# Pair columns inside an eight-field part laid out by halves, in a DLRM tower with a compressed-interaction layer

## The chip, the cores and the metric

The kernel runs on one core of a Trainium2 chip. The metric is the device time of one execution in microseconds (us). The kernel before took 377.16 us (median of 3 runs, 375.65 to 377.16).

## What is computed

For each of 1024 samples 32 rows of 32 numbers are gathered from 32 tables. From these `e` the interaction network forms products of pairs and contracts them with weights twice; the sums over the last axis go through a tower of three dense layers.

```python
e = stack([tbl_f[ids[:, f]] for f in range(32)], axis=1)     # (1024, 32, 32)
x, res = e, []
for W in (W0, W1):                                           # (1024, 128), (4096, 128)
    z = einsum('bhd,bmd->bhmd', e, x).reshape(b, 32 * x.shape[1], 32)
    x = einsum('bpd,pj->bjd', z, W)
    res.append(x)
z = sum(concatenate(res, axis=1), axis=-1)                   # (1024, 256)
h = maximum(concatenate([z, dense_ctx], 1) @ W_top1 + b_top1, 0)
h = maximum(h @ W_top2 + b_top2, 0)
y = h @ W_top3
```

All is float32.

## The kernel before

The product of field a with field b is the same as that of b with a, so the kernel works on unordered pairs, each with the sum of its two weights. The 32 fields are two sides of 16 (`HALF`), and each side two parts of 8 (`SUB`); there are four parts. The 28 pairs inside a part are 28 columns of a block of 32 (`PAIRS`), and four squares fill it up; `pair_columns` names the field pair of every column. Pairs that cross the two parts of a side have 64 columns, those that cross the sides 256 more.

**Weights.** TensorE multiplies W1, row block by row block, with the summed W0 columns (`sym`), for each of 32 fields h: 272 columns into `RT[h]`, 256 into `RX[h]` (ScalarE copies them out of PSUM). What is needed is a sum over the orders of a triple of fields, so DVE adds shifted pieces of `RX` or `RT` into `RT`, and into `QC` and `TH`, by the helper `add` (line 421, `tensor_tensor` with both inputs in SBUF). `own_adds` handles triples within a side (both inputs in `RT`), `apart_across` one part of side X against the other side, `both_across` both parts at once, `cross_first` and `cross_second` the 64 crossing columns. Each is called twice, with a first and a second round (`second`), since the second adds to what the first wrote. Then TensorE transposes the result into `C` (`weights`).

**Gathers.** GpSimd (POOL) issues 256 indirect DMAs (line 278), 8 for each of 32 units of 32 samples, one behind the other; they wait only for the index rows and for a buffer of two tiles before.

**Units.** For each unit TensorE transposes the gathered rows into the PSUM bank `ET` (`emb_transposes`), ScalarE copies `ET` to `eblk` and `eT`, DVE forms the products in `products` in three parts (`zQ` across parts, `zP` inside parts, `z3` the rest; one input is `ET` in PSUM, the other `eT` in SBUF), and TensorE contracts them (`triples`, `across_triples`, `other_triples`). ScalarE and DVE copy those results to `TS`; TensorE multiplies them with `C` (`second`, line 726). Every four units make a tile of 128 samples, and the tower follows behind each.

**Order.** Each engine's program is written out by hand, and semaphores tie them. On DVE: the first two units' products, `own_sums(0)`, `early_sums`, and then for each unit its copies, the next unit's products and, for the first three, one part of `late_sums`.

In the products inside a part, distance by distance: instruction s multiplies the fields i and i + s, for 8 - s values of i, over all parts and samples of the unit. `off(s)` is the first column of distance s. The sums go over the same columns in the same order, by distances; one more instruction does the squares in the first round.

Of the kernel before, what the change touches and what calls it, by code (L numbers as in the profile page):

```python
# [7 lines left out]
ALU = mybir.AluOpType  # L8
ACT = mybir.ActivationFunctionType

P = 128
# [3 lines left out]
HALF = 16  # L15
SUB = 8
# [7 lines left out]
Y1T = 7  # L24


def off(s):

    return sum(SUB - r for r in range(1, s))


def pair_columns():


    cols = [None] * RTC
    for p in range(4):
        f0 = SUB * p
        for s in range(1, SUB):
            for i in range(SUB - s):
                cols[32 * p + off(s) + i] = (f0 + i, f0 + i + s)  # L40
        for i in range(4):
            cols[32 * p + PAIRS + i] = (f0 + i, f0 + i)
            cols[2 * P + 4 * p + i] = (f0 + 4 + i, f0 + 4 + i)
    for X in range(2):
        for i in range(SUB):
            for k in range(SUB):
                cols[P + 64 * X + SUB * i + k] = (HALF * X + i, HALF * X + SUB + k)
    return cols


def dlrm_cin_tower(nc, dense_t, ids, bases, table, w_top1, w_dense, vec_in, w_top2, w0_cols, w0_rows, w1, out):
# [21 lines left out]
    C17 = HALF + 1  # L73
    EB = NQ * 2 * C17
    N1, N2 = H1 // P, H2 // P
    NZ = 11
    W1P = 8
    KT = 56

# [1 line left out]
    with ctx:  # L81
# [9 lines left out]
        def view(t, at, dims):  # L91

            return bass.AP(t.tensor, t.offset + at, [list(t.ap[0])] + [list(d) for d in dims])
# [325 lines left out]
        def _(eng):  # L419
            def add(dst, a, b, s):  # L420
                eng.tensor_tensor(dst, a, b, ALU.add).then_inc(s, 1)

            def rt(h, col, dims):
                return view(RT[:, :, :], RTC * h + col, dims)

            def rx(X, h, c, other, by_c, by_h, by_other):
# [2 lines left out]
                dims = [[to_c, by_c]] + [[RAB * a + to_other * b, n] for a, b, n in zip(by_h[0::2], by_other, by_h[1::2])]  # L429
                return view(RX[:, :, :], RAB * (HALF * X + h) + to_c * c + to_other * other, dims)  # L430

            def th(c, x, dims):
                return view(TH[:, :, :], THIRD * c + x, dims)

            def apart_across(X, e, c0, cn, second, s_done):

                for s in range(1, SUB) if second else range(0, SUB):  # L440
                    n = SUB - s if s else 4
                    dst = rt(HALF * (1 - X) + c0, 32 * (2 * X + e) + (off(s) if s else PAIRS), [[RTC, cn], [1, n]])
                    h, other = (s, 0) if second else (0, s)
                    add(dst, dst, rx(X, SUB * e + h, c0, SUB * e + other, cn, (1, n), (1,)), s_done)

            def both_across(X, c0, cn, second, s_done):

                for s in range(1, SUB) if second else range(0, SUB):
                    n = SUB - s if s else 4
                    dst = rt(HALF * (1 - X) + c0, 64 * X + (off(s) if s else PAIRS), [[RTC, cn], [32, 2], [1, n]])  # L450
                    h, other = (s, 0) if second else (0, s)
                    add(dst, dst, rx(X, h, c0, other, cn, (SUB, 2, 1, n), (SUB, 1)), s_done)

            def cross_first(X, c0, cn, s_done):

# [8 lines left out]
            def own_adds(X, e, second):  # L464


                f, c = (SUB, 1) if e == 0 else (1, SUB)
                for s in range(1, SUB) if second else range(0, SUB):
                    n = SUB - s if s else 4
                    dst = rt(HALF * X + SUB * (1 - e), 32 * (2 * X + e) + (off(s) if s else PAIRS), [[RTC, SUB], [1, n]])  # L470
                    h, other = (s, 0) if second else (0, s)
                    add(dst, dst, rt(HALF * X + SUB * e + h, P + 64 * X + f * other, [[c, SUB], [RTC + f, n]]),
                        (own_added if second else own_first)[X])

            def rest_across(X):

# [15 lines left out]
            def own_sums(X):  # L492
                for e in range(2):
                    own_adds(X, e, False)
                eng.wait_ge(own_first[X], 2 * SUB)
                for e in range(2):
                    own_adds(X, e, True)

            def early_sums():


                eng.wait_ge(rt_kept, HALF + SUB)
                eng.wait_ge(rx_kept, (HALF + SUB) // 2)
                both_across(0, 0, SUB, False, early_first)
                cross_first(0, 0, SUB, early_first)
                apart_across(1, 0, 0, HALF, False, early_first)
                cross_first(1, 0, HALF, late_first)
                eng.wait_ge(early_first, 2 * SUB + 1)
                both_across(0, 0, SUB, True, added)
                cross_second(0, 0, SUB, added)  # L510
                apart_across(1, 0, 0, HALF, True, added)

            def late_sums(part):
                if part == 0:
                    eng.wait_ge(rt_kept, F)
                    eng.wait_ge(rx_kept, F // 2)
                    both_across(0, SUB, SUB, False, late_first)
                    cross_first(0, SUB, SUB, late_first)
                    apart_across(1, 1, 0, HALF, False, late_first)
                    for X in range(2):  # L520
                        rest_across(X)
                        rest_own(X)
                        rest_same(X)
                if part == 1:
                    own_sums(1)
                if part == 2:
                    eng.wait_ge(late_first, 2 * SUB + 2)
                    both_across(0, SUB, SUB, True, added)
                    cross_second(0, SUB, SUB, added)
                    apart_across(1, 1, 0, HALF, True, added)  # L530
                    cross_second(1, 0, HALF, added)
# [7 lines left out]
            def products(u, part):  # L539

                parts, sides = 4 * GROUPS, 2 * GROUPS
                within, across, rest = zP[u % 2][:, :, :], zQ[u % 2][:, :, :, :], z3[u % 2][:, :, :]

                def apart(s):
                    some = [[SUB, parts], [1, SUB - s]]
                    eng.tensor_tensor(view(within, off(s), [[32, parts], [1, SUB - s]]), field(0, some), copied(s, some),  # L546
                                      ALU.mult).then_inc(z_made, 1)

                if part == 0:
                    eng.wait_ge(eblk_made, (NQ + 1) * (u + 1))  # L550
                    wait(eng, t3_made, u - 1)
                    eng.tensor_tensor(view(across, 0, [[64, sides], [SUB, SUB], [1, SUB]]),  # L552
                                      field(0, [[HALF, sides], [1, SUB], [0, SUB]]),
                                      copied(SUB, [[HALF, sides], [0, SUB], [1, SUB]]), ALU.mult).then_inc(z_made, 1)
                if part == 1:
                    for s in range(1, 5):
                        apart(s)
                if part == 2:
                    for s in range(5, SUB):
                        apart(s)  # L560
                    some = [[SUB, parts], [1, 4]]
                    eng.tensor_tensor(view(within, PAIRS, [[32, parts], [1, 4]]), field(0, some), copied(0, some),
                                      ALU.mult).then_inc(z_made, 1)
                    some = [[F, GROUPS], [SUB, 4], [1, 4]]
                    eng.tensor_tensor(view(rest, 0, [[THIRD, GROUPS], [4, 4], [1, 4]]), field(4, some), copied(4, some),
                                      ALU.mult).then_inc(z_made, 1)
                    eng.tensor_copy(view(rest, MORE, [[THIRD, GROUPS], [1, HALF]]), field(0, [[F, GROUPS], [1, HALF]]))\
                       .then_inc(z_made, 1)
# [64 lines left out]
        def _(eng):  # L633
# [14 lines left out]
            def weights(q):  # L648

                bank = WA[:, :] if q % 2 else M[:, :, :].rearrange("p a b -> p (a b)")  # L650
                if q == 0:
                    eng.wait_ge(added, 4 * (SUB - 1) + 9)
                    for X in range(2):
                        eng.wait_ge(own_added[X], 2 * (SUB - 1))
                wait(eng, c_kept, q - 1)
                for x in range(4):
                    kt = 4 * q + x
                    if kt < F:
                        piece = RT[:, kt, 0:P]
                    elif kt < F + HALF:  # L660
                        piece = QC[:, kt - F, :]
                    else:
                        n = 4 * (kt - F - HALF)
                        piece = TH[:, n:n + 4, :].rearrange("p c x -> p (c x)")
                    m = eng.transpose(bank[:, P * x:P * x + P], piece, ident[:, :])
                m.then_inc(c_made, 1)
# [209 lines left out]
```

## Time and profile before

| what | us |
|---|---|
| median of 3 runs | 377.16 |
| the profiled execution's own time | 377.52 |
| its span | 375.7 |
| PE busy (matmul) | 323.7 |
| POOL busy | 252.3 |
| ACT busy | 233.9 |
| DVE busy | 203.2 |

The span runs from the first to the last instruction. The page and the timeline give each instruction by its line, its engine and its tiles, with the elements per partition; starts are counted from the span's start. DVE instructions overlap: the next starts before the length given for one is over, so the step from start to start is what one costs. A row of the timeline with "x8" is a merged run of eight. The granted clock of TensorE was 0.982 of full speed over the span.

### The profile page before, as it was taken

The page shows a single profiled execution, that of the slowest core. Times are in us where ns is not written, and L with a number is a line of the kernel's source. Part 1 is how long each engine was busy: PE and PEld are TensorE (multiplying, and loading weights), DVE is VectorE, ACT ScalarE, POOL GpSimd, SP SyncE. Part 2 cuts the span into 40 slices and gives each one's busy share as a digit, 9 for nine tenths or more (in the row PEclk, how much of TensorE's full clock was granted, in tenths as well). Part 3 has the DMA queues.
Part 4 walks back from the last instruction along what each step waited for, and adds up shares of the span by engine and source line. Part 5 has one row for each costly group of instructions (what it writes and reads, how often), then busy time and mean ns, then how long its engine had stood idle before and what let it go on. Part 6 is the DMA issues. An engine that isn't in the chain of part 4 may idle for free.

```text
span 375.7 us, 11560 instructions
## 1 busy us (share of the span) xinstructions
PE 323.7 (86%) x4680; PEld 298.8 (80%) x4680; DVE 203.2 (54%) x834; ACT 233.9 (62%) x774; POOL 252.3 (67%) x262
## 2 busy tenths in 40 slices
PE   1899936249998999899989998998699879989897
PEld 1677735248998999899989988988698878889797
DVE  4336999933665565555646663655455544554201
ACT  1578566187667766776686667666676557556601
POOL 5777887877777777777777777777777777740000
PEclk9999996699999999999999999999999999999999
DMA  7801001010100010000101000100010001100000
GB/s 220 312 14 16 11 9 16 9 16 14 16 16 16 14 16 16 16 16 15 16 13 17 15 17 15 15 15 15 15 16 14 16 15 17 15 10 2 3 2 0
DMA packets 10773, 9.79 MB, mean 26 GB/s; under 512 B 4664, under 2 KB 8896, under 8 KB 10720
## 3 DMA queue, kind: packets, MB, share of 16 engines
q0 software_dynamic: 8192, 4.21, 7.5%
q1 hardware_dynamic: 2528, 4.84, 3.8%
q8 instruction: 37, 0.61, 0.7%
q14 instruction: 16, 0.13, 0.1%
HBM read 9.03 MB, written 0.00 MB: 24 GB/s over the span
## 4 chain that ended last, share of the span: by engine, by line
POOL 66%; issue 21%; PE 10%; DMA 1%; ACT 1%; POOLq 0%; DVE 0%; SPq 0%
POOL emb L278 66%; PE WA L726 4%; PE M L739 1%; PE PA L687 1%; DMA emb<-in_table,rows 1%; PE QB L698 1%; DMA base<-in_bases 1%; PE M L758 1%; PE M L749 0%; POOLq L81 0%; ACT h L358 0%; PE T L711 0%; PE T L787 0%; PE M L750 0%; PE ET L787 0%
## 5 line engine op out<-in xcount | busy, mean ns | idle before, releaser
L278 POOL DMA_INDIRECT emb<-in_table,rows x256 | 251.6, 983 | 80.4 <-issue 77.8
L726 PE MATMUL WA<-TS,RX 128*128 128x128 f32 x896 | 111.0, 277 | 1.0 <-ACT TS L285 1.0
L726 PEld LDWEIGHTS WA<-TS,RX 128*128 128x128 f32 x896 | 104.6, 192 | 4.1 <-issue 4.0
L584 DVE COPY TS<-T 32x64 f32<-32x64 f32 x256 | 55.5, 217 | 76.7 <-PE T L711 69.7
L285 ACT ACTIVATE eblk<-ET 32x256 f32<-32x256 f32 x128 | 48.7, 380 | 55.3 <-PE ET L674 53.0
L687 PE MATMUL PA<-eblk,zP 128*128 128x132 f32 x512 | 75.0, 282 | 1.9 <-ACT TS L285 1.1
L552 DVE TENSOR_TENSOR zQ<-ET,eT 128x1024 f32<-128x1024 f32 x32 | 39.2, 1225 | 65.2 <-ACT eT L285 65.1
L285 ACT ACTIVATE TS<-T 32x64 f32<-32x64 f32 (+1 forms) x320 | 66.5, 208 | 7.7
L687 PEld LDWEIGHTS PA<-eblk,zP 128*128 128x128 f32 x512 | 66.7, 195 | 2.7 <-ACT TS L285 1.3
L546 DVE TENSOR_TENSOR zP<-ET,eT 128x224 f32<-128x224 f32 (+6 forms) x224 | 47.7, 289 | 0.0
L285 ACT ACTIVATE TS<-PA 128x396 f32<-128x396 f32 (+1 forms) x96 | 44.5, 463 | 2.7 <-PE PA L687 1.6
L698 PE MATMUL QB<-eblk,zQ 128*32 128x68 f32 x2048 | 37.5, 224 | 0.0
L698 PEld LDWEIGHTS QB<-eblk,zQ 128*32 128x32 f32 x2048 | 32.1, 109 | 4.0 <-issue 0.2
L639 PE MATMUL PA<-sym,TS 128*128 128x272 f32 x64 | 21.2, 415 | 8.9 <-DMA TS<-in_W 7.7
L711 PE MATMUL T<-eblk,z 128*32 128x132 f32 x512 | 20.8, 279 | 4.8 <-DVE TS L587 3.5
L674 PE MATMUL ET<-ident,emb 128*128 128x128 f32 x64 | 13.4, 293 | 12.2 <-DMA emb<-in_table,rows 9.5
L285 ACT ACTIVATE TS<-QB 128x272 f32<-128x272 f32 x64 | 22.1, 408 | 0.0
L758 PE MATMUL M<-h,wt 128*128 128x128 f32 x112 | 14.4, 281 | 8.7 <-ACT h L358 8.7
L639 PEld LDWEIGHTS PA<-sym,TS 128*128 128x128 f32 x64 | 12.2, 198 | 11.3 <-issue 7.6
L758 PEld LDWEIGHTS M<-h,wt 128*128 128x128 f32 x112 | 13.0, 191 | 10.1 <-ACT h L358 10.1
L285 ACT ACTIVATE RT<-PA 128x272 f32<-128x272 f32 x32 | 12.6, 395 | 13.3 <-PE PA L639 13.2
L674 PEld LDWEIGHTS ET<-ident,emb 128*128 128x128 f32 x64 | 7.7, 146 | 15.1 <-DMA emb<-in_table,rows 11.8
(87 smaller groups left out, 290.5 us busy)
## 6 DMA issues: line engine op xcount, KB each, us to landing
emb<-in_table,rows POOLq DMA_INDIRECT x256, 2.4
TS<-in_W SPq DMA_DIRECT2D x8, 256.0 KB, 5.6
wt<-in_W_top SPq DMA_DIRECT2D x2, 512.0 KB, 8.3
y1w<-in_W_rows SPq DMA_DIRECT2D x1, 448.0 KB, 6.7
TS<-in_W_rows SPq DMA_DIRECT2D x1, 448.0 KB, 7.3
sym<-in_W_cols SPq DMA_DIRECT2D x1, 264.0 KB, 3.0
TS<-in_W_cols SPq DMA_DIRECT2D x1, 264.0 KB, 3.3
idc<-in_ids SPq DMA_DIRECT2D x1, 128.0 KB, 2.1
```

The source lines that it names most:

```text
L278: eng.indirect_dma_start(emb[par][:, g, :], None, table, bass.IndirectOffsetOnAxis(rows[:, k, g:g + 1], 0))\
L285: return eng.activation(dst, src, ACT.Copy)
L546: eng.tensor_tensor(view(within, off(s), [[32, parts], [1, SUB - s]]), field(0, some), copied(s, some), ALU.mult).then_inc(z_made, 1)
L552: eng.tensor_tensor(view(across, 0, [[64, sides], [SUB, SUB], [1, SUB]]), field(0, [[HALF, sides], [1, SUB], [0, SUB]]), copied(SUB, [[HAL ...
L584: eng.tensor_copy(view(ts[32 * q:32 * q + 32, :, :], P * REST + b0, [[4 * P, 2], [P, 4], [1, 8]]), view(src, q, [[C17, 2], [4, 4], [C33, 8 ...
L639: eng.matmul(PA[h % 2][:, 0:RTC], w1s[:, h, :], sym[:, 0:RTC], start=True, stop=True).then_inc(rt_made, 1)
L674: t = eng.transpose(ET[:, P * q:P * q + P], emb[k % 2][:, g:g + NQ, :].rearrange("p g d -> p (g d)"), ident[:, :])
L687: m = eng.matmul(PA[t % 2][:, NQ * C33 * x:NQ * C33 * x + NQ * C33].rearrange("p (v c) -> p v c", c=C33), zP[u % 2][:, g, :], eblk[u % 2][ ...
L698: m = eng.matmul(QB[g // 4][32 * j:32 * j + 32, at:at + NQ * C17].rearrange("p (v c) -> p v c", c=C17), zQ[u % 2][:, g, X, y0:y0 + 32], eb ...
L711: m = eng.matmul(T3[32 * j:32 * j + 32, at:at + NQ * C33].rearrange("p (v c) -> p v c", c=C33), z3[u % 2][:, g, :], eblk[u % 2][:, g, :, 1 ...
L726: m = eng.matmul(WA[:, 0:P], C[:, kt, :], TS[k % 2][:, slot_of(kt), :], start=(kt == 0), stop=(kt == KT - 1))
L758: m = eng.matmul(M[:, a, :], wt2[:, c, cols], h1[:, c, :], start=(c == 0), stop=(c == N1 - 1))
```

## The change

The 28 columns of a part are laid out in another order: 16 pairs of the fields 0 to 3 with 4 to 7, then 4 pairs of the fields 0, 1 with 2, 3, and 4 of 4, 5 with 6, 7, then the four neighbour pairs (0, 1), (2, 3), (4, 5), (6, 7). Each of these four groups is one instruction (a table `BLOCKS` gives the start column, first field and width), where the order by distances takes seven. The host lays out the weights by the same `pair_columns`. In `both_across` the pattern of a group of width 4 or 2 has no dimension left for the two parts, so these stand in a loop over parts. The count `NZ` of a unit's product instructions goes from 11 to 8, and the counts that are waited for change with it.

```diff
-def off(s):
-    return sum(SUB - r for r in range(1, s))
+def part_pairs():
+    pairs = [(a, 4 + b) for a in range(4) for b in range(4)]
+    pairs += [(4 * n + a, 4 * n + 2 + b) for n in range(2) for a in range(2) for b in range(2)]
+    pairs += [(2 * j, 2 * j + 1) for j in range(4)]
+    return pairs
...
-    NZ = 11
+    NZ = 8
+    BLOCKS = ((0, 0, 4), (HALF, 0, 2), (HALF + 4, 4, 2), (HALF + SUB, 0, 1))
...
+            def steps(w, by_first, by_second):
+                if w == 1:
+                    return [[2 * (by_first + by_second), 4]]
+                return [[by_first, w], [by_second, w]]
+
+            def pairs_at(w):
+                return [[1, 4]] if w == 1 else [[w, w], [1, w]]
+
             def apart_across(X, e, c0, cn, second, s_done):
-                for s in range(1, SUB) if second else range(0, SUB):
-                    n = SUB - s if s else 4
-                    dst = rt(HALF * (1 - X) + c0, 32 * (2 * X + e) + (off(s) if s else PAIRS), [[RTC, cn], [1, n]])
-                    h, other = (s, 0) if second else (0, s)
-                    add(dst, dst, rx(X, SUB * e + h, c0, SUB * e + other, cn, (1, n), (1,)), s_done)
+                to_c, to_other = (1, HALF) if X == 0 else (HALF, 1)
+                row, col = HALF * (1 - X) + c0, 32 * (2 * X + e)
+                for at, f, w in BLOCKS:
+                    dst = rt(row, col + at, [[RTC, cn]] + pairs_at(w))
+                    h, other = (f + w, f) if second else (f, f + w)
+                    by = (to_other, RAB) if second else (RAB, to_other)
+                    add(dst, dst, rx_at(X, SUB * e + h, c0, SUB * e + other, [[to_c, cn]] + steps(w, *by)), s_done)
+                if not second:
+                    dst = rt(row, col + PAIRS, [[RTC, cn], [1, 4]])
+                    add(dst, dst, rx_at(X, SUB * e, c0, SUB * e, [[to_c, cn], [RAB + to_other, 4]]), s_done)
...
             def both_across(X, c0, cn, second, s_done):
...
+                    if w == 1:
+                        dst = rt(row, col + at, [[RTC, cn], [32, 2]] + pairs_at(w))
+                        add(dst, dst, rx_at(X, h, c0, other, [[to_c, cn], [SUB * (RAB + to_other), 2]] + steps(w, *by)), s_done)
+                    else:
+                        for e in range(2):
+                            dst = rt(row, col + 32 * e + at, [[RTC, cn]] + pairs_at(w))
+                            add(dst, dst, rx_at(X, SUB * e + h, c0, SUB * e + other, [[to_c, cn]] + steps(w, *by)), s_done)
...
                 if part == 1:
-                    for s in range(1, 5):
-                        apart(s)
+                    eng.tensor_tensor(view(within, 0, [[32, parts], [4, 4], [1, 4]]), field(0, [[SUB, parts], [1, 4], [0, 4]]),
+                                      copied(4, [[SUB, parts], [0, 4], [1, 4]]), ALU.mult).then_inc(z_made, 1)
+                    for g in (0, 4):
+                        eng.tensor_tensor(view(within, HALF + g, [[32, parts], [2, 2], [1, 2]]), field(g, [[SUB, parts], [1, 2], [0, 2]]),
+                                          copied(g + 2, [[SUB, parts], [0, 2], [1, 2]]), ALU.mult).then_inc(z_made, 1)
                 if part == 2:
-                    for s in range(5, SUB):
-                        apart(s)
+                    eng.tensor_tensor(view(within, HALF + SUB, [[32, parts], [1, 4]]), field(0, [[SUB, parts], [2, 4]]),
+                                      copied(1, [[SUB, parts], [2, 4]]), ALU.mult).then_inc(z_made, 1)
```

`own_adds` is changed like `apart_across`.

On DVE, in `early_sums`, the instructions of one part across the sides (`apart_across(1, 0, ...)`, the `128x16...` rows) stood between the two `cross_first` (the `...x64` rows) like this before:

```order
L421 TENSOR_TENSOR RT<-RT,RX 128x8x64
L421 TENSOR_TENSOR RT<-RT,RX 128x16x4
L421 TENSOR_TENSOR RT<-RT,RX 128x16x7
L421 TENSOR_TENSOR RT<-RT,RX 128x16x6
L421 TENSOR_TENSOR RT<-RT,RX 128x16x5
L421 TENSOR_TENSOR RT<-RT,RX 128x16x4
L421 TENSOR_TENSOR RT<-RT,RX 128x16x3
L421 TENSOR_TENSOR RT<-RT,RX 128x16x2
L421 TENSOR_TENSOR RT<-RT,RX 128x16
L421 TENSOR_TENSOR RT<-RT,RX 128x16x64
```

In the changed program the same place, with the eight instructions of `both_across` ahead of it (the `128x8...` rows), reads:

```order
L425 TENSOR_TENSOR RT<-RT,RX 128x8x16 x2
L425 TENSOR_TENSOR RT<-RT,RX 128x8x4 x4
L425 TENSOR_TENSOR RT<-RT,RX 128x8x2x4 x2
L425 TENSOR_TENSOR RT<-RT,RX 128x8x64
L425 TENSOR_TENSOR RT<-RT,RX 128x16x16
L425 TENSOR_TENSOR RT<-RT,RX 128x16x4 x4
L425 TENSOR_TENSOR RT<-RT,RX 128x16x64
```

Eight instructions of 112 down to 16 elements became one of 256 and four of 64; nothing else moved between them.

On DVE, a unit's products before (`zQ` across parts, `zP` inside, `z` the rest):

```order
L552 TENSOR_TENSOR zQ<-ET,eT 128x1024
L546 TENSOR_TENSOR zP<-ET,eT 128x32x7
L546 TENSOR_TENSOR zP<-ET,eT 128x32x6
L546 TENSOR_TENSOR zP<-ET,eT 128x32x5
L546 TENSOR_TENSOR zP<-ET,eT 128x32x4
L546 TENSOR_TENSOR zP<-ET,eT 128x32x3
L546 TENSOR_TENSOR zP<-ET,eT 128x32x2
L546 TENSOR_TENSOR zP<-ET,eT 128x32
L562 TENSOR_TENSOR zP<-ET,eT 128x32x4
L565 TENSOR_TENSOR z<-ET,eT 128x8x16
L567 COPY z<-ET 128x8x16
```

and in the changed program:

```order
L584 TENSOR_TENSOR zQ<-ET,eT 128x1024
L588 TENSOR_TENSOR zP<-ET,eT 128x32x16
L591 TENSOR_TENSOR zP<-ET,eT 128x32x4 x2
L594 TENSOR_TENSOR zP<-ET,eT 128x32x4
L597 TENSOR_TENSOR zP<-ET,eT 128x32x4
L600 TENSOR_TENSOR z<-ET,eT 128x8x16
L602 COPY z<-ET 128x8x16
```

Seven instructions with 896 elements became four with the same 896.

## Rows read from the trace of the kernel before

**Rows 1.** The page: the chain that ended last, and the costliest group.

```profile
POOL emb L278 66%; PE WA L726 4%; PE M L739 1%; PE PA L687 1%; DMA emb<-in_table,rows 1%; PE QB L698 1%; DMA base<-in_bases 1%; PE M L758 1%; PE M L749 0%; POOLq L81 0%; ACT h L358 0%; PE T L711 0%; PE T L787 0%; PE M L750 0%; PE ET L787 0%
...
L278 POOL DMA_INDIRECT emb<-in_table,rows x256 | 251.6, 983 | 80.4 <-issue 77.8
```

**Rows 2.** The gathers' own line: duration min/median/max, first and last start.

```profile
L278 POOL DMA_INDIRECT emb<-in_table,rows x256: 943/947/2323, 4.1 to 332.5; - x128
```

**Rows 3.** Timeline, end of the gathers: start, length, engine, operation, [idle before].

```profile
332.50 0.95 POOL L278 DMA_INDIRECT emb<-in_table,rows  x1 [0.31 <-issue]
334.90 0.44 PE L674 MATMUL ET<-ident,emb 128*128 128x128 f32 x2 [1.03 <-DMA emb<-in_table,rows]
...
338.55 1.49 DVE L546 TENSOR_TENSOR zP<-ET,eT 128x224 f32<-128x224 f32 x7
...
340.34 0.28 DVE L567 COPY z<-ET 128x128 f32<-128x128 f32 x1
...
343.58 0.84 PE L687 MATMUL PA<-eblk,zP 128*128 128x132 f32 x6
```

**Rows 4.** Timeline, middle of the run: a unit's last gather, and its transposes.

```profile
192.43 0.95 POOL L278 DMA_INDIRECT emb<-in_table,rows  x1 [0.30 <-issue]
...
198.78 0.38 PE L674 MATMUL ET<-ident,emb 128*128 128x128 f32 x2
```

**Rows 5.** Line of the transposes from 200 us on: what PE idled for, us, times.

```profile
  DMA emb<-in_table,rows: 8.1, 9
```

**Rows 6.** Groups of POOL's instructions between 30 and 80 us: busy, mean ns, idle.

```profile
L278 POOL DMA_INDIRECT emb<-in_table,rows x34 | 40.9, 1204 | 10.4 <-issue 10.4
```

**Rows 7.** Timeline of POOL: seven of the slow gathers.

```profile
5.52 1.45 POOL L278 DMA_INDIRECT emb<-in_table,rows  x1 [0.30 <-issue]
...
37.68 1.69 POOL L278 DMA_INDIRECT emb<-in_table,rows  x1 [0.31 <-issue]
...
41.21 1.97 POOL L278 DMA_INDIRECT emb<-in_table,rows  x1 [0.30 <-issue]
43.48 2.11 POOL L278 DMA_INDIRECT emb<-in_table,rows  x1 [0.30 <-issue]
...
49.78 2.12 POOL L278 DMA_INDIRECT emb<-in_table,rows  x1 [0.30 <-issue]
...
69.06 2.32 POOL L278 DMA_INDIRECT emb<-in_table,rows  x1 [0.30 <-issue]
71.69 1.59 POOL L278 DMA_INDIRECT emb<-in_table,rows  x1 [0.30 <-issue]
```

**Rows 8.** Timeline of DVE, windows cut so that single instructions and blocks stand.

```profile
5.44 0.71 DVE L594 TENSOR_TENSOR sym<-sym,TS 128x528 f32<-128x528 f32 x1 [1.61 <-DMA TS<-in_W_cols]
...
34.68 4.04 DVE L421 TENSOR_TENSOR RT<-RT 128x32 f32<-128x32 f32 x30
...
38.63 1.53 DVE L421 TENSOR_TENSOR RT<-RT,RX 128x64 f32<-128x64 f32 x8
...
40.09 1.03 DVE L421 TENSOR_TENSOR RT<-RT,RX 128x512 f32<-128x512 f32 x1
...
42.25 0.22 DVE L421 TENSOR_TENSOR RT<-RT,RX 128x32 f32<-128x32 f32 x1
42.38 0.17 DVE L421 TENSOR_TENSOR RT<-RT,RX 128x16 f32<-128x16 f32 x1
42.48 1.21 DVE L421 TENSOR_TENSOR RT<-RT,RX 128x1024 f32<-128x1024 f32 x1
43.62 1.36 DVE L421 TENSOR_TENSOR RT<-RT,RX 128x112 f32<-128x112 f32 x7
...
44.80 0.17 DVE L421 TENSOR_TENSOR RT<-RT,RX 128x16 f32<-128x16 f32 x1
44.89 1.11 DVE L421 TENSOR_TENSOR QC<-RT,RX 128x512 f32<-128x512 f32 x1
...
70.57 1.88 DVE L421 TENSOR_TENSOR QC<-RT,RX 128x1024 f32<-128x1024 f32 x1
```

More of the change, by code:

```diff
@@ L37, in pair_columns @@
         f0 = SUB * p
-        for s in range(1, SUB):
-            for i in range(SUB - s):
-                cols[32 * p + off(s) + i] = (f0 + i, f0 + i + s)
+        for n, (a, b) in enumerate(part_pairs()):
+            cols[32 * p + n] = (f0 + a, f0 + b)
         for i in range(4):
@@ L430, in rx, with rx_at @@
                 return view(RX[:, :, :], RAB * (HALF * X + h) + to_c * c + to_other * other, dims)
+            def rx_at(X, h, c, other, dims):
+                to_c, to_other = (1, HALF) if X == 0 else (HALF, 1)
+                return view(RX[:, :, :], RAB * (HALF * X + h) + to_c * c + to_other * other, dims)
             def th(c, x, dims):
                 return view(TH[:, :, :], THIRD * c + x, dims)
-            def apart_across(X, e, c0, cn, second, s_done):
-                for s in range(1, SUB) if second else range(0, SUB):
-                    n = SUB - s if s else 4
-                    dst = rt(HALF * (1 - X) + c0, 32 * (2 * X + e) + (off(s) if s else PAIRS), [[RTC, cn], [1, n]])
-                    h, other = (s, 0) if second else (0, s)
-                    add(dst, dst, rx(X, SUB * e + h, c0, SUB * e + other, cn, (1, n), (1,)), s_done)
@@ L446, in both_across @@
-            def both_across(X, c0, cn, second, s_done):
[L448 to L452, printed above, removed]
+            def steps(w, by_first, by_second):
+                if w == 1:
+                    return [[2 * (by_first + by_second), 4]]
+                return [[by_first, w], [by_second, w]]
@@ new lines, in pairs_at @@
+            def pairs_at(w):
+                return [[1, 4]] if w == 1 else [[w, w], [1, w]]
+            def apart_across(X, e, c0, cn, second, s_done):
+                to_c, to_other = (1, HALF) if X == 0 else (HALF, 1)
+                row, col = HALF * (1 - X) + c0, 32 * (2 * X + e)
[7 more added lines that the diff above has]
+                    add(dst, dst, rx_at(X, SUB * e, c0, SUB * e, [[to_c, cn], [RAB + to_other, 4]]), s_done)
@@ new lines, in both_across @@
+            def both_across(X, c0, cn, second, s_done):
+                to_c, to_other = (1, HALF) if X == 0 else (HALF, 1)
+                row, col = HALF * (1 - X) + c0, 64 * X
+                for at, f, w in BLOCKS:
+                    h, other = (f + w, f) if second else (f, f + w)
+                    by = (to_other, RAB) if second else (RAB, to_other)
+                    if w == 1:
[5 more added lines that the diff above has]
+                            add(dst, dst, rx_at(X, SUB * e + h, c0, SUB * e + other, [[to_c, cn]] + steps(w, *by)), s_done)
+                if not second:
+                    dst = rt(row, col + PAIRS, [[RTC, cn], [32, 2], [1, 4]])
+                    add(dst, dst, rx_at(X, 0, c0, 0, [[to_c, cn], [SUB * (RAB + to_other), 2], [RAB + to_other, 4]]), s_done)
@@ L467, in own_adds @@
                 f, c = (SUB, 1) if e == 0 else (1, SUB)
[L468 to L473, printed above, removed]
+                row, col, s_done = HALF * X + SUB * (1 - e), 32 * (2 * X + e), (own_added if second else own_first)[X]
+                for at, g, w in BLOCKS:
+                    h, other = (g + w, g) if second else (g, g + w)
+                    by = (f, RTC) if second else (RTC, f)
+                    dst = rt(row, col + at, [[RTC, SUB]] + pairs_at(w))
+                    add(dst, dst, rt(HALF * X + SUB * e + h, P + 64 * X + f * other, [[c, SUB]] + steps(w, *by)), s_done)
+                if not second:
+                    dst = rt(row, col + PAIRS, [[RTC, SUB], [1, 4]])
+                    add(dst, dst, rt(HALF * X + SUB * e, P + 64 * X, [[c, SUB], [RTC + f, 4]]), s_done)
             def rest_across(X):
@@ L494, in own_sums @@
                     own_adds(X, e, False)
-                eng.wait_ge(own_first[X], 2 * SUB)
+                eng.wait_ge(own_first[X], 2 * 5)
                 for e in range(2):
@@ L507, in early_sums @@
                 cross_first(1, 0, HALF, late_first)
-                eng.wait_ge(early_first, 2 * SUB + 1)
+                eng.wait_ge(early_first, 8 + 1 + 5)
                 both_across(0, 0, SUB, True, added)
@@ L526, in late_sums @@
                 if part == 2:
-                    eng.wait_ge(late_first, 2 * SUB + 2)
+                    eng.wait_ge(late_first, 1 + 8 + 1 + 5)
                     both_across(0, SUB, SUB, True, added)
@@ L542, in products @@
                 within, across, rest = zP[u % 2][:, :, :], zQ[u % 2][:, :, :, :], z3[u % 2][:, :, :]
[L544 to L547, printed above, removed]
                 if part == 0:
@@ L651, in weights @@
                 if q == 0:
-                    eng.wait_ge(added, 4 * (SUB - 1) + 9)
+                    eng.wait_ge(added, 2 * 7 + 2 * 4 + 9)
                     for X in range(2):
-                        eng.wait_ge(own_added[X], 2 * (SUB - 1))
+                        eng.wait_ge(own_added[X], 2 * 4)
                 wait(eng, c_kept, q - 1)
```

## The prediction

> **What bounds the kernel now.** I read the page's chain of waits first: 66% of the span is the issue of the gathers on POOL, line 278 [rows 1]. The 256 gathers start between 4.1 and 332.5 us; one takes 0.947 us by the median, but the slowest 2.32 [rows 2], and 0.30 of idle lies between two [rows 7]. So 1.25 us each is the pace, and the last gather starts at 332.50. The timeline at that end shows TensorE idle 1.03 us for it, its transposes at 334.90, and then work on PE without a hole that the changed engine makes [rows 3]. From there to the end of the span is 375.7 - 334.9 = 40.8 us of TensorE work that the diff doesn't touch.
>
> Is TensorE near enough to become the bound if gathers come earlier? In the middle of the run it is late: the gather that ended at 193.38 got its transposes at 198.78 [rows 4]. From 200 us on it has caught up, and idles 8.1 us in 9 waits for gathers [rows 5]. So gathers may come some 8 us earlier and the end follows one for one; if they come later, it follows at once.
>
> DVE doesn't set the end by its own length: the last unit's products end at 340.34 + 0.28 = 340.62, and PE first needs them at about 343.6 [rows 3], 2.9 us later. **DVE matters through another door.** Between 30 and 80 us there are 34 gathers with 40.9 us busy [rows 6]; at the median it would be 34 x 0.947 = 32.2. These 8.7 us are nearly all of the excess of the run (251.6 - 256 x 0.947 = 9.2, [rows 1]). The slow ones stand where DVE does the additions of line 421 [rows 7, 8].
>
> When does a slow gather get on? The addition of 5.44 us ends at 6.15, the gather that began inside it at 6.97 [rows 7, 8]: 0.82 after. Take 0.82 off the ends of the gathers of 41.21, 43.48 and 69.06, and each falls beside the start of a DVE addition: 42.36 (a start at 42.38), 44.77 (44.80) and 70.56 (70.57). For the first two the instruction just ended has 32 elements a partition, for the last 16; the gather of 43.48 has by then let pass the boundaries behind 112, 96, 80, 64 and 48 elements, all of one block of seven [rows 7, 8]; the gather of 71.69 waits for the end of the 1024, 72.45, behind which a copy from PSUM comes. So a waiting gather gets in only behind a short addition or behind one that doesn't read SBUF twice. Behind 32 elements it is not always so: the gather of 69.06 passes the one behind 32 and gets in behind 16, at the start of the 1024 (70.57).
>
> The Trainium skill, "SBUF — State Buffer", section "SBUF: two separate sides", says that a VectorE instruction with two SBUF inputs and a GpSimd operation that reads SBUF exclude each other for the whole instruction, whichever starts first. That they exclude each other, the trace agrees; but by that rule alone the gather of 43.48 would go on at the next boundary, after about 0.1 us, and it took 2.11 us in place of 0.947 [rows 7]. A run of additions back to back keeps the port here, so I price the change by lengths of runs. What it would be by the rule stands as a rival.
>
> **Price of an addition.** Seven instructions, 448 elements, from 43.62 to 44.89: 1.27 us; one of 16 elements, from 42.38 to 42.48: 0.10 [rows 8]. Solving gives about 0.065 us an instruction and 0.0018 us an element with strided inputs. The 1024 contiguous from 42.48 to 43.62: 1.14, so 0.00105 an element [rows 8].
>
> **The change, part by part.**
> - Products: 11 instructions of a unit become 8, elements unchanged: 3 x 0.065 = 0.2 us in each of 32 units, 6.2 us of DVE. All of it lies beside waits: in the last unit the cover is the 2.9 us above. Price 0. If the new patterns (stride 0 inside four, stride 2) ran at 0.0018 in place of 0.00105, the 896 elements cost 0.7 more and are still covered. If the cover were gone, the last unit would give -0.2 or cost up to 0.5.
> - Own sums: 30 instructions to 18 in each half; they take 34.68 to 38.63, 3.95 us [rows 8], so 12 x 0.065 = 0.8 less, twice.
> - Sums of one part across (four blocks, two with eight instructions and two with seven): to five and four. First: 8 x 0.065 + 512 x 0.0018 = 1.44; now 5 x 0.065 + 256 x 0.00105 + 256 x 0.0018 = 1.05, since the 4 by 4 and 2 by 2 read neighbours. Second: 1.26 to 1.07. Together 1.2 us less.
> - Sums of both parts across: eight and seven instructions before and after, same elements: 0. But sizes change from 64, 112 down to 16, to two of 128, four of 32, one or two of 64.
> - No wait is added; the counts that are waited for follow the new numbers of instructions.
>
> So the additions shrink by about 2.8 us. By itself this moves nothing on the path; the port does. In the new order no addition of 16 or 8 elements is left. Within a block of both parts there are four of 32 in a row; within a block of one part only 256 and 64s; the products by halves (512, 1024) follow right behind.
>
> **Walk through the new stretch**, taking that a gather gets in behind 32 but not behind 64. Own sums start at 34.5 and end at 37.65, with so many of 32 that they hold up a gather little. Then: two of 128 to 38.25, four of 32 to 38.7, 64s to 39.1, 512 (0.96) to 40.05, one part to 41.1, 1024 to 42.25, 128s to 42.8, 32s to 43.3, 64 to 43.5, 512 to 44.5, one part to 45.6, 128s to 46.2, 32s to 46.7, 64s, 512 and one part to 49.05, the rest to the first copy at 49.5. Gathers get in at about 38.5, 42.95, 46.3 and 49.5: three steps in 11.0 us, where the pace asks 3.75, so 7.2 lost. Before, in the same work, the gathers from that of 37.68 to that of 49.78 (three more stand between those shown) get in from 38.55 to 51.08 [rows 7]: six steps in 12.5 us, 5.0 lost. The last part: one gets in among the 32s, the next only at the end behind one part and the 1024, 4.2 us later: 3.0 lost; before, 2.1 (69.06 and 71.69: 1.37 and 0.64, a third 0.1) [rows 7]. The own sums: before 8.7 - 5.0 - 2.1 = 1.6; after, by my choice, half of it, 0.8, since they have so many 32s. Sum 11.0 against 8.7: +2.3 us.
>
> The profiled execution took 377.52; 379.8 with this. The median of the runs lies 0.36 lower, 377.16, so I forecast **379.5 us**. Its own range, by the phase in which gathers meet the runs (one step is 1.25) and by 32 not always letting one in: 377.5 to 382.
>
> **Rivals.**
> 1. *Shorter additions, shorter lock.* The loss goes with the time of the additions: they took 17.4 in one stretch from 34.68 us, 3.95 for the second own sums and, by the prices above, 1.27 + 1.04 + 1.26 + 1.8 = 5.4 in the last part, 26.7 us in all for 8.7 lost, 0.32 each; 2.8 less give -0.9: 376.3. For it: the simplest reading. Against: the ends that fall behind short ones.
> 2. *Behind 64 too.* In the walk gathers then get in also within the blocks of one part (near 40.6, 45.2, 48.6, and 66.7 in the last part): 6.4 lost, -2.3: 375. Against: in the blocks of [rows 7, 8] none did. With every boundary open, as the whole-instruction rule has it, about 4.3 are lost, -4.4: 373. That is the lower end.
> 3. *Only behind 24 or less, on the other side further out.* Then nothing opens the run between 37.7 and 49.5 us, nor that of the last part: one gather in 11.8 us, 10.5 lost, 4 in the last part, 2 in the own sums: +7.8, 385. It decides if a waiting gather lets pass most of the 32s; the gather of 69.06 did once, two others didn't.
> 4. *DVE's own time counts*: 32 x 0.2 = 6.2 us less, 371. Against: the 2.9 us of cover and the gathers' pace.
>
> **How the numbers follow.** Forecast 0.42, of it 0.1 ends within 0.5%; rival 1 0.18; rival 2 with every boundary 0.20; rival 3 0.18; rival 4 0.02. A measurement of this kernel tells 0.5%, 1.9 us, from no change. Faster 0.22, same 0.18 + 0.10 = 0.28, slower 0.50. The range, from every boundary open to nothing behind 32: 373.3 to 385.5; the likeliest's own is given above.
>
> **What would show it.** The gathers' line between 30 and 80 us: fewer than 34 starts, mean above 1204 ns, single ones of 3 us and more near 39 to 42 and 65 to 69; their ends less 0.82 behind additions of 32. The start of the last gather near 334.8, transposes 2.4 later, and still 40.8 to the end. The adds of one part at 1.05 us, a unit's within-part products near 1.2. I am wrong if the last gather starts before 332.5, if gathers get in behind 64s or 256s, or if the tail behind the last transposes changes.

## The result, and the profile after

| | before | changed |
|---|---|---|
| median, us | 377.09 (375.65 to 377.16, 4 runs) | 383.46 (380.15 to 384.21, 4 runs) |
| profiled execution, its own time and span | 377.52, 375.7 | 383.21, 381.4 |
| last gather starts | 332.50 | 338.22 |
| 256 gathers busy, less 256 x 0.947 | 9.2 | 15.0 |

The ratio is 1.016, 95% interval 1.012 to 1.020: 6.4 us slower. The bound is the same and is later. The page of the changed kernel, the chain and the gathers' group (the lines that answer to [rows 1]):

```profile
POOL emb L282 67%; PE WA L761 4%; PE M L774 1%; PE PA L722 1%; DMA emb<-in_table,rows 1%; PE QB L733 1%; DMA base<-in_bases 1%; PE M L793 1%; PE M L784 0%; POOLq L85 0%; ACT h L362 0%; PE T L746 0%; PE T L822 0%; PE M L785 0%; PE ET L822 0%
...
L282 POOL DMA_INDIRECT emb<-in_table,rows x256 | 257.4, 1005 | 80.3 <-issue 77.7
```

The timeline at the end of the gathers, to be held against [rows 3] (start, length, engine, operation, [idle before]):

```profile
338.22 0.94 POOL L282 DMA_INDIRECT emb<-in_table,rows  x1 [0.30 <-issue]
...
340.55 0.44 PE L709 MATMUL ET<-ident,emb 128*128 128x128 f32 x2 [0.97 <-DMA emb<-in_table,rows]
...
344.21 0.68 DVE L588 TENSOR_TENSOR zP<-ET,eT 128x512 f32<-128x512 f32 x1
...
345.80 0.28 DVE L602 COPY z<-ET 128x128 f32<-128x128 f32 x1
...
349.25 0.84 PE L722 MATMUL PA<-eblk,zP 128*128 128x132 f32 x6
```

The last gather is 5.72 us later, the transposes 5.65, and from them to the end are 381.4 - 340.55 = 40.85 us, where it was 40.8. The products of the last unit end 0.2 us sooner after the transposes than before, and PE needs them 3.2 us later: nothing of that is seen at the end. So the whole loss lies in when the gathers were issued. Between 30 and 80 us (against [rows 6]) there are five gathers fewer, and the mean is longer:

```profile
L282 POOL DMA_INDIRECT emb<-in_table,rows x29 | 42.4, 1464 | 8.8 <-issue 8.8
```

That is 42.4 - 29 x 0.947 = 14.9 us lost there, where it was 8.7. The timeline of POOL in the stretch of the sums (against [rows 7]):

```profile
36.00 1.36 POOL L282 DMA_INDIRECT emb<-in_table,rows  x1 [0.30 <-issue]
37.66 6.57 POOL L282 DMA_INDIRECT emb<-in_table,rows  x1 [0.30 <-issue]
44.53 5.81 POOL L282 DMA_INDIRECT emb<-in_table,rows  x1 [0.30 <-issue]
50.65 0.95 POOL L282 DMA_INDIRECT emb<-in_table,rows  x1 [0.30 <-issue]
...
64.54 4.96 POOL L282 DMA_INDIRECT emb<-in_table,rows  x1 [0.30 <-issue]
```

and DVE there, merged runs (against [rows 8]):

```profile
34.98 2.98 DVE L425 TENSOR_TENSOR RT<-RT 128x128 f32<-128x128 f32 x18
37.87 5.83 DVE L425 TENSOR_TENSOR RT<-RT,RX 128x128 f32<-128x128 f32 x22
43.62 1.06 DVE L425 TENSOR_TENSOR QC<-RT,RX 128x512 f32<-128x512 f32 x1
44.59 4.47 DVE L425 TENSOR_TENSOR RT<-RT,RX 128x256 f32<-128x256 f32 x18
48.98 0.36 DVE L425 TENSOR_TENSOR TH<-RT,RX 128x128 f32<-128x128 f32 x1
49.26 0.26 DVE L425 TENSOR_TENSOR TH<-RT 128x64 f32<-128x64 f32 x1
49.44 0.18 DVE L526 COPY TH<-RT 128x64 f32<-128x64 f32 x1
...
66.77 1.90 DVE L425 TENSOR_TENSOR QC<-RT,RX 128x1024 f32<-128x1024 f32 x1
68.57 0.94 DVE L619 COPY TS<-T 32x64 f32<-32x64 f32 x4
```

The reader is to see three gathers of 5 to 6.6 us (three more took 1.0 to 1.4) where the kernel before had thirteen slow ones of 1.0 to 2.3. The end of each less 0.82 is where it gets on, as in the prediction. These are 43.41, 49.52 and 68.68: the first behind the last of four additions of 32 elements (a step of 0.149 where the other three take 0.12), the second at the end of a copy, the third when the 1024 is over and a copy from PSUM comes. DVE itself became shorter, as was worked out: own sums 2.9 us for 3.95, the stretch to the first copy from PSUM 15.15 us (34.98 to 50.13) for 17.5.

From the instruction starts of five traces (the kernel before, the changed one in two profiles, and the two below that add short additions) I counted, for each gather later than 30 us that waited, which addition had just ended when it got in, and which ends it let pass.

| elements of the addition just ended | let pass | got in |
|---|---|---|
| 8 | 0 | 14 |
| 16 | 1 | 6 |
| 24 | 2 | 1 |
| 32, contiguous inputs (a step of 0.10 to 0.13) | 4 | 9 |
| 32, strided inputs, kernel before | 7 | 3 |
| 32, strided inputs, the four other traces | 55 | 4 |
| 40 to 1024, an addition following | 163 | 1 |

("Contiguous" are the additions of 32 that one experiment below adds; "strided" are all of the sums. Of the four entries in the last but one row, one was at a wait for a semaphore. Entries behind a 1024 that a copy from PSUM follows are left out of the last row.)

### The profile page after: what moved, and what is told of

The parts are those of the page before. It is cut to its first block, busy times and chain, and to the rows that moved or that the text cites. A ratio compares the mean times of both kernels' runs of the same rounds, so it can differ in the third digit from the quotient of the medians.

```text
span 381.4 us, 11428 instructions
## 1 busy us (share of the span) xinstructions
PE 327.9 (86%) x4680; PEld 301.6 (79%) x4680; DVE 192.7 (51%) x702; ACT 234.1 (61%) x774; POOL 258.0 (68%) x262
## 4 chain that ended last, share of the span: by engine, by line
POOL 67%; issue 21%; PE 10%; DMA 1%; ACT 1%; POOLq 0%; DVE 0%; SPq 0%
POOL emb L282 67%; PE WA L761 4%; PE M L774 1%; PE PA L722 1%; DMA emb<-in_table,rows 1%; PE QB L733 1%; DMA base<-in_bases 1%; PE M L793 1%; PE M L784 0%; POOLq L85 0%; ACT h L362 0%; PE T L746 0%; PE T L822 0%; PE M L785 0%; PE ET L822 0%
## 5 line engine op out<-in xcount | busy, mean ns | idle before, releaser
L282 POOL DMA_INDIRECT emb<-in_table,rows x256 | 257.4, 1005 | 80.3 <-issue 77.7
L722 PE MATMUL PA<-eblk,zP 128*128 128x132 f32 x512 | 75.9, 284 | 1.9 <-ACT TS L289 1.1
L722 PEld LDWEIGHTS PA<-eblk,zP 128*128 128x128 f32 x512 | 67.5, 197 | 2.7 <-ACT TS L289 1.5
L588 DVE TENSOR_TENSOR zP<-ET,eT 128x512 f32<-128x512 f32 x32 | 21.8, 681 | 0.0
```

Source lines behind the costliest of these rows:

```text
L282: eng.indirect_dma_start(emb[par][:, g, :], None, table, bass.IndirectOffsetOnAxis(rows[:, k, g:g + 1], 0))\
L588: eng.tensor_tensor(view(within, 0, [[32, parts], [4, 4], [1, 4]]), field(0, [[SUB, parts], [1, 4], [0, 4]]), copied(4, [[SUB, parts], [0, ...
L722: m = eng.matmul(PA[t % 2][:, NQ * C33 * x:NQ * C33 * x + NQ * C33].rearrange("p (v c) -> p v c", c=C33), zP[u % 2][:, g, :], eblk[u % 2][ ...
```

## The experiments

All times are medians beside runs of the kernel before on the same chip; "lost" is the gathers' busy time on the page less 256 x 0.947.

| kernel | median, us | ratio to before, interval | lost |
|---|---|---|---|
| changed, memset behind each addition | 372.49 | 0.987 (0.983 to 0.991) | 4.5 |
| before, memset behind each addition | 370.14 | 0.981 (0.977 to 0.985) | 1.0 |
| changed, additions are memsets | 368.24 | 0.977 (0.973 to 0.980) | 0.6 |
| before, additions are memsets | 368.68 | 0.978 (0.974 to 0.981) | 0.7 |
| changed, memset behind each block | 373.24 | 0.988 (0.981 to 0.995) | 4.9 |
| changed, addition of 8 behind each block | 374.60 | 0.994 (0.990 to 0.998) | 5.9 |
| changed, addition of 32 behind each block | 377.45 | 0.999 (0.995 to 1.003) | 10.2 |
| changed, additions are copies | 373.57 | 0.989 (0.982 to 0.996) | 5.3 |
| changed, memsets and crossings cut | 369.86 | 0.979 (0.976 to 0.982) | 1.2 |
| before, memset behind each block | 373.29 | 0.988 (0.984 to 0.991) | 3.8 |
| changed, again | 382.64 | 1.010 (1.006 to 1.015) | 15.6 |

**An opening behind each addition.** The edit, the same in both kernels:

```diff
+            def door():
+                at = next(doors)
+                eng.memset(spare[:, at:at + 1], 0.0)
...
                 eng.tensor_tensor(dst, a, b, ALU.add).then_inc(s, 1)
+                door()
```

> The changed kernel with a memset of one element (no SBUF input) behind each addition of the sums; nothing else is changed. Theory (back-to-back additions with two SBUF inputs keep the port, and a gather gets in behind anything that isn't one): no gather waits longer than the addition it meets, so none takes above 0.95 + 1.9 us; all together they lose 3 to 5 us in place of 15, the last gather starts near 327 to 329 us, time 370.5 to 373. Rival (the gathers lose in proportion to the time that DVE spends on the sums): DVE's stretch becomes some 6 us longer, so 384 or more. Rival (the loss comes from something else in the new layout): 383, unchanged.

> The kernel before with the same memset behind each of its additions. Theory: loss 3 to 5 us in place of 8.7, last gather near 327 to 329, time 371 to 373.5. Rival (in proportion to DVE's time): about 140 more instructions, 379 or more. Rival (the layout alone makes the difference): 377, unchanged.

DVE of the changed kernel with memsets, from its timeline:

```profile
38.31 0.20 DVE L432 TENSOR_TENSOR RT<-RT,RX 128x32 f32<-128x32 f32 x1
38.32 0.06 DVE L429 MEMSET spare<- 128x1 f32 x1
38.44 0.20 DVE L432 TENSOR_TENSOR RT<-RT,RX 128x32 f32<-128x32 f32 x1
38.45 0.06 DVE L429 MEMSET spare<- 128x1 f32 x1
38.57 0.20 DVE L432 TENSOR_TENSOR RT<-RT,RX 128x32 f32<-128x32 f32 x1
```

and its gathers:

```profile
38.65 0.95 POOL L283 DMA_INDIRECT emb<-in_table,rows  x1 [0.30 <-issue]
39.91 1.17 POOL L283 DMA_INDIRECT emb<-in_table,rows  x1 [0.30 <-issue]
41.38 1.85 POOL L283 DMA_INDIRECT emb<-in_table,rows  x1 [0.31 <-issue]
43.54 1.03 POOL L283 DMA_INDIRECT emb<-in_table,rows  x1 [0.30 <-issue]
```

More instructions and less time, in both kernels, as the theory had it. The changed kernel came out inside its expectation: 372.49 us, 4.5 lost, the last gather at 327.68, the longest 2.52 us. The 4.5 are also near the 4.3 that the prediction's rival 2 had worked out for every boundary open. The memset starts 0.01 us after the addition, and the step from one addition of 32 to the next is 0.13 with it, 0.125 without: an opening costs DVE next to nothing. What is left is lost at the long additions: a gather started inside five of the changed kernel's six of 512 and 1024 elements, and these five gathers took 1.17 to 2.52 us.

The kernel before with memsets was faster than expected (370.14 for 371 to 373.5), and lost 1.0 for the 3 to 5 expected, with the same six long additions. There each of the six began 0.14 to 0.44 us after a gather had, and that gather took 0.94 to 0.97; the next one came in the last 0.2 us of the addition or behind it and took 1.08 at most, but for one of 1.61. Two gathers and the addition between them:

```profile
45.66 0.95 POOL L279 DMA_INDIRECT emb<-in_table,rows  x1 [0.30 <-issue]
45.80 1.08 DVE L428 TENSOR_TENSOR QC<-RT,RX 128x512 f32<-128x512 f32 x1
46.91 1.08 POOL L279 DMA_INDIRECT emb<-in_table,rows  x1 [0.30 <-issue]
```

So the 3.5 us between the two losses lie in how the gathers' starts fell against the long additions, in one profile of each kernel. Whether the layout makes them fall so, or chance, isn't shown. The last gather of the kernel before with memsets starts at 324.25, but its span is 369.2, 45.0 later and not 43.2: TensorE no longer waits for gathers (its waits for them are 1.2 us in one, where the changed kernel with memsets has 5.2 in six), its last transposes begin 4.2 us after the last gather (328.48) with PE busy ahead of them, and it has become the bound.

**No SBUF inputs at all.** In both kernels:

```diff
-                eng.tensor_tensor(dst, a, b, ALU.add).then_inc(s, 1)
+                eng.memset(dst, 0.0).then_inc(s, 1)
```

> The changed kernel in which every addition of the sums is a memset of the same output (same number of instructions, same semaphores, no SBUF input; the weights that are computed are left out by this). Theory: no gather is slow behind 30 us, the last starts near 324, time 367.5 to 369.5. Rival (the products' new patterns or a later TensorE cost something too): more than 370, and more than its twin from the kernel before.

> The kernel before in which every addition of the sums is a memset of the same output (the weights that are computed are left out by this). Theory: 367.5 to 369.5, and within 0.5 us of the changed kernel with memsets, so that the port is the whole difference of the two kernels and the products give nothing. Rival (the shorter products are worth something and the port hid it): the changed one with memsets is 1 to 6 us faster than this one.

Between 30 and 80 us, the group of gathers of the changed kernel with memsets for additions (busy, mean ns, idle; against [rows 6]):

```profile
L282 POOL DMA_INDIRECT emb<-in_table,rows x41 | 38.8, 946 | 12.5 <-issue 12.5
```

and of its twin from the kernel before:

```profile
L278 POOL DMA_INDIRECT emb<-in_table,rows x41 | 38.7, 944 | 12.5 <-issue 12.5
```

With their instructions in the same order and no contention the two kernels are 0.4 us apart, which their runs don't separate (367.90 to 368.92 and 368.24 to 368.88), and no gather behind 30 us is slow. So the contention is the whole difference between them as far as these runs can tell, and the shorter products of 32 units give nothing like the 6.2 us of DVE time that they save. One caution for what follows: TensorE was granted a clock of 0.995 in both of these profiles, where it was 0.982 in those of the two kernels and 0.968 to 0.977 in the five with memsets between additions. So 368 us says when the gathers would let the kernel end, and not how fast TensorE would be with real weights.

**Openings behind blocks, of three kinds.** The memset, or instead of it an addition with both inputs in SBUF (`ident`), behind each of the 22 blocks of the changed kernel:

```diff
+            def door():
+                at = 8 * next(doors)
+                eng.tensor_tensor(spare[:, at:at + 8], ident[:, 0:8], ident[:, 32:32 + 8], ALU.add)
```

(with 32 in place of each 8 in the third kernel, and `eng.memset(spare[:, at:at + 1], 0.0)` in the first).

> The changed kernel with the one-element memset only behind each of the 22 blocks of additions (one part, both parts, own, or one crossing product), not behind each addition. Theory (what counts is the length of a run of additions back to back): a waiting gather gets in at the next block's end, 1 to 1.8 us away at most where it was 5; lost 5 to 8 us in place of 15, time 374 to 377. Rival (the memset helps by something other than ending a run, for instance because it delays each addition): in proportion to the memsets, 22 of 116, about 381.

> The changed kernel with one addition of 8 elements, both inputs in SBUF, into a spare tile behind each of the 22 blocks. Theory as in the prediction (a short addition lets a waiting gather in): about as with memsets at the same places, 374 to 378. Rival (only an instruction that doesn't read two SBUF inputs opens the run, and the short additions of the kernel before stood there by chance): 383 to 384.

> The same with 32 elements in place of 8. Theory (short means 16 or less; in the changed kernel gathers passed over a dozen additions of 32): 382 to 385, as without it. Rival (any addition with contiguous operands, or one more instruction, opens the run): 374 to 378, as with 8.

With additions of 8, gathers on the timeline:

```profile
38.98 1.20 POOL L283 DMA_INDIRECT emb<-in_table,rows  x1 [0.30 <-issue]
40.49 1.76 POOL L283 DMA_INDIRECT emb<-in_table,rows  x1 [0.30 <-issue]
```

and DVE:

```profile
39.28 0.15 DVE L429 TENSOR_TENSOR spare<-ident 128x8 f32<-128x8 f32 x1
39.35 1.03 DVE L432 TENSOR_TENSOR RT<-RT,RX 128x512 f32<-128x512 f32 x1
...
41.34 0.16 DVE L429 TENSOR_TENSOR spare<-ident 128x8 f32<-128x8 f32 x1
41.42 1.22 DVE L432 TENSOR_TENSOR RT<-RT,RX 128x1024 f32<-128x1024 f32 x1
```

38.98 + 1.20 - 0.82 = 39.36 and 40.49 + 1.76 - 0.82 = 41.43: each gets in just where the addition of 8 gives way to the next (39.35, 41.42), 13 of 13. So a short addition opens the run although it reads SBUF twice, and the layout by distances had such ones at the end of each block. Of 32 contiguous elements, 9 of 13 let a gather in. I had expected 382 to 385 of that kernel, and it took 377.45: "16 or less" was too strict. Of the strided 32s of the sums, in the changed kernel and its two variants here, 4 of 59 let one in.

What makes the difference is not settled. It isn't the step alone: most strided 32s take 0.12 to 0.13 us and the contiguous ones start at 0.10, but nine strided ones of the own sums took 0.10 to 0.11 too, and all nine were let pass, while the nine contiguous ones that let a gather in took 0.10 to 0.13. The added additions differ from those of the sums in more than their stride: they write a tile of their own and raise no semaphore. None of this was varied by itself.

The memsets behind blocks gave 373.24 and 4.9 lost, 0.8 us better than the lower end expected; 22 are nearly as good as one behind each addition.

**One SBUF input.** The additions of the changed kernel as copies:

```diff
-                eng.tensor_tensor(dst, a, b, ALU.add).then_inc(s, 1)
+                eng.tensor_copy(dst, b).then_inc(s, 1)
```

> The changed kernel in which every addition is a copy of its second input, SBUF to SBUF, float32 (the weights that are computed are left out by this). Theory (two SBUF inputs keep the port): no slow gathers behind 30 us, 367.5 to 369.5 as with memsets. Rival (a float32 copy within SBUF takes both ports too, as the Trainium skill, SBUF — State Buffer, section SBUF: two separate sides, has it): gathers are slow as with additions, 375 or more.

Its gathers:

```profile
36.16 1.29 POOL L282 DMA_INDIRECT emb<-in_table,rows  x1 [0.31 <-issue]
37.76 2.33 POOL L282 DMA_INDIRECT emb<-in_table,rows  x1 [0.30 <-issue]
40.39 1.76 POOL L282 DMA_INDIRECT emb<-in_table,rows  x1 [0.30 <-issue]
```

and DVE beside them:

```profile
36.91 3.22 DVE L425 COPY RT<-RX 128x128 f32<-128x128 f32 x18
```

The theory failed here: with one SBUF input gathers are slow too, 5.3 lost and 373.57 us, between the two expectations. The copies take half as long (1024 elements in 0.68 us; the addition 1.21), so the runs are shorter. That a float32 copy within SBUF keeps GpSimd from writing a DMA's descriptors is what the Trainium skill has in "SBUF — State Buffer", section "SBUF: two separate sides", and this trace agrees in that the gathers are slow (1.29 to 2.33 us above); it doesn't show the descriptors. "Two SBUF inputs" was too narrow a name for what keeps the port.

**The crossings cut.** Beside the memsets, each `cross_first` and `cross_second` in additions of 256 elements, the semaphore raised by the last:

```diff
+            def in_parts(c0, cn, one, s_done):
+                for c in range(c0, c0 + cn, 4):
+                    m = add_part(*one(c))
+                m.then_inc(s_done, 1)
```

> The changed kernel with the one-element memset behind each addition, and the crossing products (512 and 1024 elements) cut into additions of 256. Theory: the longest run is then one addition of about 0.5 us, the gathers lose 1 to 2.5 us, the last starts at 324.3 to 326, and TensorE, whose weights are ready about 4 us before those of the kernel before with memsets, still waits for gathers at the end: 368.7 to 370.3, at or under the 370.1 of that kernel. Rival (more instructions cost more than the open port gives): 371.5 or more.

> The kernel before with the one-element memset only behind each of its 22 blocks. Theory: the ends of its blocks have short additions that open the run already, so the memsets add few new openings (behind the crossing products, and behind own sums): lost 6 to 8.5 us in place of 9.1, 374.5 to 377. Rival (a memset at a block's end is worth as much here as in the changed kernel, 10 us): 372 or less.

369.86 us, 2.1% under the kernel before and 3.3% under the changed one (382.64 in the same rounds), within 0.3 us of the kernel before with memsets, from which its interval doesn't tell it apart. It loses 1.2 us, and it is still bound by gathers:

```profile
324.57 0.94 POOL L283 DMA_INDIRECT emb<-in_table,rows  x1 [0.30 <-issue]
...
326.88 0.44 PE L732 MATMUL ET<-ident,emb 128*128 128x128 f32 x2 [1.02 <-DMA emb<-in_table,rows]
```

The kernel before with memsets behind blocks only missed its expectation: 373.29 for 374.5 to 377, and 3.8 lost for 6 to 8.5. The openings behind the crossing products and at the own sums were worth 5.4 us of loss, more than I gave them.

**The changed kernel again,** with no edit, for a second profile of it.

> The changed kernel itself, timed in more rounds. Theory: the loss depends on how the gathers' pace of 1.25 us meets the runs, so the executions spread from 380 to 385 with the median near 383.4, while kernels without additions spread by under 1 us; its profile again shows two or three gathers of 4 to 7 us and nothing else slow. Rival (one unlucky profile): a median near 380 and a profile with many gathers of 2 us.

```profile
36.40 1.14 POOL L282 DMA_INDIRECT emb<-in_table,rows  x1 [0.30 <-issue]
37.85 12.94 POOL L282 DMA_INDIRECT emb<-in_table,rows  x1 [0.30 <-issue]
51.09 0.94 POOL L282 DMA_INDIRECT emb<-in_table,rows  x1 [0.30 <-issue]
...
66.11 3.98 POOL L282 DMA_INDIRECT emb<-in_table,rows  x1 [0.31 <-issue]
```

One gather of 12.94 us, the whole of `early_sums` and the late part behind it: what rival 3 of the prediction describes, nothing opening the run from 37.7 us to its end. It gets on at 50.79 - 0.82 = 49.97. The loss is 12.0 us there and 3.0 in the last part, where rival 3 had 10.5 and 4. The executions spread from 379.9 to 383.7 us, those of each kernel with memsets for additions over 1.0 or less. Neither expectation had a gather of 13 us; one (I had said two or three of 4 to 7) makes the same loss, 15.6.

## Why the prediction was right, and where it fell short

- *The bound.* Right. 40.85 us from the last transposes to the end, the gathers' delay passed on one for one: 5.72 us on POOL, 5.7 in the span.
- *The products at 0.* Right, and shown by the two kernels with memsets for additions, 0.4 us apart. The cover at the end was 3.2 us.
- *DVE's price.* Right: own sums 0.8 less in the working, 1.06 in the trace; a block of one part in its first round 0.97, from 40.24 on, for 1.05. (Solved from the two steps as the prediction prints them, an instruction is 0.073 us and a strided element 0.0017; with its 0.065 and 0.0018 the 1.27 us come out as well, and nothing hangs on the difference.)
- *The port, and length of runs in place of time.* Right in kind: shown by memsets that lengthen DVE's program and take 10 us off, and by the changed kernel losing more although its additions are shorter. Rival 1 (loss in proportion to the additions' time) and rival 2 (openings behind 64) are out: 84 of 85 ends of 64 were passed. Rival 4 is out by the two kernels of the line on the products.
- *"A gather gets in behind 32 but not behind 64"*: this is the step that failed, in the walk. The result lies nearer to rival 3 than to the forecast: 15.0 us lost, where the forecast had 11.0 and rival 3, with a chance of 0.18, 16.5; and the second profile is rival 3 in kind. Of strided 32s, 3 of 10 let one in before, and I took four in a row as an opening. That could have been read before: the prediction speaks of one 32 that was passed and two that weren't, but all the waiting gathers of the same trace had passed seven. In the four other traces 4 of 59 did. The four expected entries (38.5, 42.95, 46.3, 49.5) became two: 43.41 and 49.52. The term that was mis-sized is the loss in the long stretch: 7.2 in the working, 5.6 + 4.9 = 10.5 measured, and 3.0 against 4.0 in the last part. With 0.8 for the own sums measured as about 0.5, the sum is 15.0 where 11.0 stood, and the time 383.5 where 379.5 did. The loss moved the way that was forecast and for the reason that was given, but that it kept within the range owes much to rival 3 standing at its upper end. It is inside the range given and outside the likeliest case's own, 377.5 to 382.
- Why a 32 opened three times in the kernel before stays open. A 16 follows each of the three, and in the changed kernel a 32, 64 or 128 does; but a 16 also follows four of the seven 32s that were passed, so the next one's length doesn't settle it. What sets the three apart is their step, 0.14 us where the seven took 0.12 to 0.13, and the one at 43.41 in the changed kernel has 0.149. Whether a longer step lets the gather in, or the gather that gets in makes the step longer, these traces don't tell.

## What to carry to other kernels

Where a kernel's pace is set by gathers that GpSimd issues, what VectorE does beside them is to be priced by its runs back to back with SBUF-only inputs, the longest above all, not by its busy time or its number of instructions. Count in the trace of before how many ends of each kind a waiting gather was let pass, and not only the few where one got in. Merging small instructions into large ones can take away the gaps in which the gathers got on; a one-element memset between them gives these back at about 0.01 us each. When the gathers are freed, look for what is next: here TensorE at 370 us. Whether VectorE's own shorter time counts from there on isn't shown: the two kernels that would tell, 370.14 and 369.86 us, can't be told apart.

## What the runs showed of the hardware

- A gather of 0.947 us waited up to 12 us behind additions back to back, past more than 40 instruction ends: the end of an addition with another right behind it doesn't by itself give it a turn.
- It reaches the contested part about 0.1 us after its start and needs 0.82 us from there; a gather that began 0.1 us before an addition of 1.09 us (14.79 against 14.90, in the kernel before) was not slowed, nor were the six of the kernel before with memsets that began 0.14 to 0.44 us before an addition of 512 or 1024 elements (0.94 to 0.97 us).
- A memset of one element starts 0.01 us after the addition ahead of it has started, costs 0.01 in the step, and still opens the run. The gather then gets in some 0.07 us after the next addition has started (42.41 against 42.35 in the changed kernel), where it does so at that start behind an addition of 8. A copy of 64 elements within SBUF opened it once (49.52) and was let pass once: in the second profile of the changed kernel the same copy ends at 49.29, and the gather got in only at 49.97, just after the first copy from PSUM started (49.89).
- Additions with strided second input cost about 0.0018 us an element beside some 0.065 an instruction (448 elements in seven: 1.27 us), contiguous ones 0.00105 (1024 elements: 1.14 us).
